# A vision tower, a two-way state-space layer and a mixture of experts in one kernel: three image pairs in flight per loop pass, both images of a pair in one instruction, and B and C rows spread by DMA

## The reference, cut to what matters

```python
x = patch_embed(images)                     # 16x16 patches: 196 tokens and a class token, 128 channels
for l in range(2):                          # two transformer layers, 8 heads of 16
    h = rmsnorm(x, ln1)
    attn = softmax((q @ k.T) / 4)           # 197 x 197 per head
    x = x + (attn @ v) @ wo.T
    h2 = rmsnorm(x, ln2)
    x = x + (silu(h2 @ wg.T) * (h2 @ wu.T)) @ wd.T   # 344 wide
h = rmsnorm(x, ln_f)
# state-space layer, forward and backward in time, 16 states per channel
dA  = exp(dt[..., None] * A)
dBx = dt[..., None] * Bm[:, :, None, :] * xs[..., None]
hst = scan(dA, dBx)                         # h[t] = dA[t] * h[t-1] + dBx[t]
y   = (einsum('blds,bls->bld', hst, Cm) + D * xs) * silu(z)
h = layernorm(h + out_f + out_b)
# 64 experts, 8 per token, at most 256 tokens per expert over the whole batch
h = layernorm(h + moe(h))
```

## Time and profile before

| what | value |
|---|---|
| median of 3 runs | 12895.33 us (12876.94 to 12912.05) |
| profiled execution, span from first to last instruction | 13032.3 us |
| median over span | 0.9895 |
| DVE busy over the span | 8016.1 us, 62% |
| PE busy over the span | 8924.6 us, 68% |
| ACT busy over the span | 5903.0 us, 45% |
| POOL busy over the span | 2489.9 us, 19% |
| mean granted PE clock, share of full speed | 0.779 |

### The profile page before, as it was taken

One profiled execution on the slowest core, in us unless ns is written; L12 is line 12 of the kernel. 1 busy time (PEld: TensorE's weight loads), 2 busy tenths in 40 slices (PEclk: granted clock), 3 DMA queues, 4 the chain that ended last, 5 costly groups with the idle time before them and its releaser, 6 DMA issues. The chain is left out here.

```text
span 13032.3 us, 153093 instructions
## 1 busy us (share of the span) xinstructions
PE 8924.6 (68%) x48772; PEld 5897.0 (45%) x48772; DVE 8016.1 (62%) x13143; ACT 5903.0 (45%) x13164; POOL 2489.9 (19%) x1809
## 2 busy tenths in 40 slices
PE   5656566577777777777777777777777777777642
PEld 3434344344444444444444444444444444444421
DVE  3556566566666666666666666666666666666724
ACT  4334343444544454445444544445444544454411
POOL 0222222211111111111111111111111111111164
PEclk8777777787878888878878887878787878888755
DMA  2000000000000000000000000000000000000034
GB/s 88 7 11 6 12 6 8 10 10 5 10 10 10 5 10 10 10 6 9 10 10 10 5 10 10 10 5 10 10 10 5 10 10 10 6 9 10 2 53 111
DMA packets 130841, 183.68 MB, mean 14 GB/s; under 512 B 27033, under 2 KB 112893, under 8 KB 121469
## 3 DMA queue, kind: packets, MB, share of 16 engines
q1 hardware_dynamic: 95068, 150.00, 3.6%
q0 software_dynamic: 34816, 21.19, 1.2%
HBM read 113.96 MB, written 57.12 MB: 13 GB/s over the span
## 5 line engine op out<-in xcount | busy, mean ns | idle before, releaser
L478 POOL TENSOR_TENSOR hs<-hs 128x788 f32<-128x788 f32 x512 | 949.7, 1855 | 7866.3 <-DVE hs L904 7866.3
L608 ACT ACTIVATE P<-psS,least_s 99x197 f32<-99x197 f32 x4096 | 1394.7, 428 | 1437.9 <-DVE least_s L791 1437.0
L1109 PE MATMUL psS<-KM,Q 128*99 128x394 f32 x4096 | 1757.9, 549 | 162.0 <-issue 61.9
L897 DVE TENSOR_TENSOR_SCAN hs<-dA,hs 128x1576 f32<-128x1576 f32 x512 | 1763.9, 3445 | 27.5
L1123 PE MATMUL psS<-cst,P 99*99 99x99 f32 x8192 | 1108.5, 288 | 818.9 <-ACT P L608 762.8
L692 ACT ACTIVATE dA<-dt_,aneg 128x394 f32<-128x394 f32 x2048 | 1179.4, 617 | 682.5 <-DVE hs L897 682.5
L1123 PEld LDWEIGHTS psS<-cst,P 99*99 99x99 f32 x8192 | 963.7, 194 | 1133.1 <-ACT P L608 1047.3
L1219 PE MATMUL psA<-bc,bcsel_h 96*128 96x394 bf16 x2048 | 786.1, 384 | 800.4 <-DVE hs L904 624.0
L791 DVE TENSOR_REDUCE least_s<-psS 99x4 f32<-99x788 f32 x1024 | 991.2, 973 | 278.6 <-PE psS L1109 265.7
L1109 PEld LDWEIGHTS psS<-KM,Q 128*99 128x99 f32 x4096 | 729.7, 187 | 703.9 <-issue 536.0
L575 ACT ACTIVATE sq<-X 128x197 f32<-128x197 f32 x640 | 228.5, 366 | 1780.3 <-DVE X L824 1140.3
(11 more groups left out here) (203 smaller groups left out, 15631.5 us busy)
## 6 DMA issues: line engine op xcount, KB each, us to landing
pat<-patches SPq DMA_DIRECT2D x64, 1176.0 KB
rows_scratch<-zeros SPq DMA_DIRECT2D x1, 19104.0 KB, 61.9
hs<-sum_scratch SPq DMA_DIRECT2D x24, 512.0 KB, 3.5
out<-hs SPq DMA_DIRECT2D x24, 512.0 KB, 2.6
sum_scratch<-HW SPq DMA_DIRECT2D x64, 148.5 KB
slot_scratch<-toki,sloti POOLq DMA_INDIRECT x320
dA<-w SPq DMA_DIRECT2D x32, 128.0 KB
sum_scratch<-HW SPq DMA_DIRECT2D x64, 48.5 KB
```

Source lines behind the costliest of these rows:

```text
L478: nc.gpsimd.tensor_tensor(hs[:, g % HBUF, 0:2, :], hs[:, g % HBUF, 0:2, :], hs[:, g % HBUF, 2:4, :], ALU.add).then_inc(half_summed, 1)
L608: last = nc.scalar.activation(P[:, b, m, 0:T], psS[0:CT, 2 * b + m // 2, m % 2 * T:(m % 2 + 1) * T], ACT.Exp, bias=least_s[:, b, m:m + 1], ...
L897: nc.vector.tensor_tensor_scan(h, dA[:, g % 2, :, :].rearrange("p n t -> p (n t)"), h, 0.0, ALU.mult, ALU.add).then_inc(scan_ready, 1)
L1109: last = mm(psS[0:CT, 2 * b + j, 0:2 * T].rearrange("p (e t) -> p e t", e=2), Q[:, b, q * CT:(q + 1) * CT], KM[:, b, m:m + 2, 0:T], start= ...
```

## The change

The diff rewrites the main loop; the experts and the closing norm keep their work and their order.

1. **Three pairs per pass.** The front half is cut into two roles. Role 0 does patch embedding and layer 0 of one pair, role 1 does layer 1 and the last norm of the pair before it, and the units do the state-space layer of the pair before that. `role_stages` lists a role's stages; the 101 stages of both are merged by position, role 1 with a lag of 2.5 stages. X has three buffers, and the other tensors of the front half are indexed by role instead of by image.
2. **Merged images.** Stages outside the attention rounds handle both images in one instruction (394 columns for 197). A role has eight rounds of two heads and a half of the queries, still one image at a time, so that each instruction of a round is half as wide: one score matmul of 394, a minimum over 2x197, two exponentials, four transposes, a copy of 396. The count of score matmuls, exponentials and transposes over a pass stays.
3. **B and C by DMA.** `xproj` is one matmul with 64 output rows (32 for dt, 32 for B and C). Its B and C rows are written to DRAM (`share`, SP queue), and each group's four B rows and four C rows are read back to all 128 partitions by one DMA each (`load`). The selector matmuls and `split` are gone. Inputs and outputs are one DVE instruction of 4x394 per group.
4. **Sums.** The first addition of a group moves from POOL to DVE (`half`); the second is now a second identity matmul on PE.
5. **Masked keys** are made on ACT as 16 copies of 396 with a per-partition scale (`keys`), not on DVE and POOL.
6. **Tables.** New `WEIGHT` and `COST`, the same for all engines. By `shares()` the first input unit stands behind stage 43 of 101 (counted from 0); everything up to the eighth decay of a pass stands before it, the eight scans, outputs and halves and seven of the eight inputs after it.

```diff
+UNITS = [("patch",), ("project", 0, 0), ("-sum", QUARTERS - 1), ("project", 0, 1), ("project", 1, 0), ("conv", 0), ("-ys", 1),
+         ("project", 1, 1), ("-merge",), ("keep",), ("conv", 1), ("sigmoid", 0), ("leave",), ("-route",), ("-store",),
+         ("sigmoid", 1), ("gate", 0), ("gate", 1), ("xproj", 0), ("share", 0), ("load", 0), ("load", 1), ("xproj", 1),
+         ("share", 1), ("load", 2), ("dtproj", 0), ("dt", 0), ("dtproj", 1), ("dt", 1)]
+UNITS += [("decay", g, k) for g in range(2) for k in range(QN)] + [("input", 0)]
 for _g in range(QUARTERS):
-    for _k in range(QN):
-        UNITS += [("decay", 1, _k)] if _g == 0 else []
-        UNITS += [("input", _g, _k)]
-    UNITS += [("scan", _g)] + ([("sum", _g - 1)] if _g else [])
-    for _k in range(QN):
-        UNITS += [("decay", _g + 2, _k)] if _g + 2 < QUARTERS else []
-        UNITS += [("output", _g, _k)]
...
-COST = {"project": 2, "conv": 2, "sigmoid": 2, "gate": 3, "xproj": 2.55, "split": 2.88, "dtproj": 0.65, "dt": 4,
-        "decay": 0.3, "input": 0.5, "scan": 2, "output": 0.5, "sum": 0.61, "merge": 4, "keep": 0.3, "leave": 0,
...
+def role_stages(r):
+    out = [("conv", 0)] if r == 0 else []
+    out += [("square", r, 0), ("norm", r, 0), ("qkv", r), ("keys", r, 0)]
+    for n in range(ROUNDS):
+        out += [("score", r, n, b) for b in range(G)]
+        out += [("keys", r, n + 1)] if n + 1 < HP else []
+        out += [("value", r, 0)] if n == HP else []
+        out += [("turn", r, n, b) for b in range(G)]
+    out += [("value", r, 1), ("den", r), ("wo", r), ("square", r, 1), ("norm", r, 1), ("gate", r), ("sig", r), ("up", r), ("down", r)]
+    out += [("square", r, 2), ("norm", r, 2)] if r else []
+    return out
...
+LAG = 2.5
...
+        "input": 1.7, "scan": 3.4, "half": 0.9, "output": 1.7, "sum": 0.6, "ys": 1, "merge": 4, "keep": 0.3, "leave": 0,
...
+                for k, (name, r, *args) in enumerate(STAGES):
+                    i = (ahead, front)[r]
+                    if i is not None and name in stages:
+                        stages[name](i, r, *args)
+                    if back is not None:
+                        until(SHARE[k])
+            run(0, None, None)
+            run(1, 0, None)
+            run(2, 1, 0)
+            with eng.Fori(0, STEPS - 3 - peel) as i:
+                run(i + 3, i + 2, i + 1)
+            for i in range(STEPS - 2 - peel, STEPS - 2):
+                run(i + 2, i + 1, i)
+            run(None, STEPS - 1, STEPS - 2)
...
+            def share(i, d):
+                if d == 0 and not is_first(i):
+                    q.wait_ge(mul_done, i * MULS)
+                    q.sem_inc(q_waited, 1)
+                if d == 0:
+                    q.wait_ge(xs_ready, i * 2 + 2)
+                    q.sem_inc(q_waited, 1)
+                q.wait_ge(dtbc_ready, i * 2 + d + 1)
+                q.dma_start(bc_d[d], dtbc[DTR:DTR + 2 * NS, d, :]).then_inc(bc_stored, 16)
...
+            def load(i, g):
+                d, n = divmod(g, QUARTERS // 2)
+                if n == 0:
+                    q.wait_ge(bc_stored, i * 32 + d * 16 + 16)
+                    q.sem_inc(q_waited, 1)
+                if g >= HBUF or not is_first(i):
+                    q.wait_ge(acc_done, i * QUARTERS + g - HBUF + 1 if g >= HBUF else i * QUARTERS)
+                q.dma_start(hs[:, g % HBUF, :, :], bc_d[d:d + 1, n * QN:(n + 1) * QN, :].to_broadcast([128, QN, N])).then_inc(b_loaded[g % HBUF], 16)
+                if g >= CBUF or not is_first(i):
+                    q.wait_ge(mul_done, i * MULS + MUL_OUT[g - CBUF] if g >= CBUF else i * MULS)
+                q.dma_start(cr[:, g % CBUF, :, :], bc_d[d:d + 1, NS + n * QN:NS + (n + 1) * QN, :].to_broadcast([128, QN, N])).then_inc(c_loaded[g % CBUF], 16)
             q.sem_inc(hw_free, 1)
...
-            def sum_(i, g):
-                pool.wait_ge(mul_done, i * MULS + (g + 1) * 2 * QN)
-                nc.gpsimd.tensor_tensor(hs[:, g % HBUF, 0:2, :], hs[:, g % HBUF, 0:2, :], hs[:, g % HBUF, 2:4, :], ALU.add).then_inc(half_summed, 1)
-                pool.wait_ge(half_summed, i * QUARTERS + g + 1)
-                nc.gpsimd.tensor_tensor(hs[:, g % HBUF, 0, :], hs[:, g % HBUF, 0, :], hs[:, g % HBUF, 1, :], ALU.add).then_inc(summed, 1)
...
+            def keys(i, r, h):
+                act.wait_ge(kq_done[r], i * 2 + 1)
+                for k in (2 * h, 2 * h + 1):
+                    last = nc.scalar.activation(KM[:, r, k, :, :].rearrange("p g t -> p (g t)"), psG[:, r, 0:2 * TP], ACT.Copy, scale=c("heads", k, k + 1))
+                last.then_inc(km_ready[r], 1)
...
+            def turn(i, r, n, b):
+                h = n % HP
+                act.wait_ge(round_done[r], i * ROUNDS * 4 + n * 4 + 2 + b + 1)
+                nc.scalar.activation(PT[:, r, b, 2 * h:2 * h + 2, :, :].rearrange("p h c t -> p (h c t)"), psS[0:CT, 2 * r + b, 0:2 * TP], ACT.Copy).then_inc(p_ready[r], 1)
...
-            def input_(i, g, k):
-                m = 2 * QN * g + k
-                if k == 0 and g >= HBUF:
-                    dve.wait_ge(acc_done, i * QUARTERS + g - HBUF + 1)
-                dve.wait_ge(bb_done, i * MULS + m + 1)
-                nc.vector.tensor_tensor(hs[:, g % HBUF, k, :], u[:, g // (QUARTERS // 2), :], AB[m % 2][:, 0:N], ALU.mult).then_inc(mul_done, 1)
+                nc.vector.tensor_tensor(u[:, d, :], dt_[:, d, :], XZ[:, d, 0, :], ALU.mult).then_inc(u_ready, 1)
+            def input_(i, g):
+                d = g // (QUARTERS // 2)
+                dve.wait_ge(b_loaded[g % HBUF], ring(i, g, HBUF))
+                dve.wait_ge(u_ready, i * 2 + d + 1)
+                nc.vector.tensor_tensor(hs[:, g % HBUF, :, :], hs[:, g % HBUF, :, :], u[:, d, :].unsqueeze(1).to_broadcast([128, QN, N]), ALU.mult).then_inc(mul_done, 1)
...
-            def output(i, g, k):
-                m = 2 * QN * g + QN + k
-                if k == 0:
-                    dve.wait_ge(scan_ready, i * QUARTERS + g + 1)
-                dve.wait_ge(bb_done, i * MULS + m + 1)
-                nc.vector.tensor_tensor(hs[:, g % HBUF, k, :], hs[:, g % HBUF, k, :], AB[m % 2][:, 0:N], ALU.mult).then_inc(mul_done, 1)
...
+            def output(i, g):
+                dve.wait_ge(scan_ready, i * QUARTERS + g + 1)
+                dve.wait_ge(c_loaded[g % CBUF], ring(i, g, CBUF))
+                nc.vector.tensor_tensor(hs[:, g % HBUF, :, :], hs[:, g % HBUF, :, :], cr[:, g % CBUF, :, :], ALU.mult).then_inc(mul_done, 1)
+            def half(i, g):
+                dve.wait_ge(mul_done, i * MULS + MUL_OUT[g])
+                nc.vector.tensor_tensor(hs[:, g % HBUF, 0:2, :], hs[:, g % HBUF, 0:2, :], hs[:, g % HBUF, 2:4, :], ALU.add).then_inc(half_summed, 1)
...
+            def score(i, r, n, b):
+                q, h = divmod(n, HP)
+                if n == 0:
+                    (pe.wait_ge(q_ready[r], i + 1), pe.wait_ge(v_ready[r], i + 1))[b]
+                else:
+                    pe.wait_ge(p_ready[r], i * ROUNDS * 4 + (n - 1) * 4 + 2 + b + 1)
+                if q == 0 and b == 0:
+                    pe.wait_ge(km_ready[r], i * HP + h + 1)
+                mm(psS[0:CT, 2 * r + b, 0:2 * T].rearrange("p (e t) -> p e t", e=2), Q[:, r, b, q * CT:(q + 1) * CT], KM[:, r, 2 * h:2 * h + 2, b, 0:T], start=True, stop=True).then_inc(round_done[r], 1)
...
-            def broadcast(i, g, m, row):
-                d = g // (QUARTERS // 2)
-                if m == 0:
-                    pe.wait_ge(bcs_ready, i * 2 + 2)
-                if m >= 2:
-                    pe.wait_ge(mul_done, i * MULS + m - 1)
-                mm(AB[m % 2][:, 0:N], bcsel[:, row, :], bc[:, d, :], start=True, stop=True).then_inc(bb_done, 1)
...
             def sum_(i, g):
                 d, q = divmod(g, QUARTERS // 2)
                 if q == 0:
                     pe.wait_ge(dt_ready, i * 2 + 2) if d == 0 else pe.wait_ge(ys_ready, i * 2 + 1)
-                pe.wait_ge(summed, i * QUARTERS + g + 1)
-                mm(psY[:, 0:N], c("ident"), hs[:, g % HBUF, 0, :], start=q == 0, stop=False).then_inc(acc_done, 1)
+                pe.wait_ge(half_summed, i * QUARTERS + g + 1)
+                for k in range(2):
+                    last = mm(psY[:, 0:N], c("ident"), hs[:, g % HBUF, k, :], start=q == 0 and k == 0, stop=False)
+                last.then_inc(acc_done, 1)
                 if q == QUARTERS // 2 - 1:
```

804 lines of the change are left out of this document (330 added, 474 removed), and 3 rows, old and new, of the table WEIGHT.

## The result

| | before | changed |
|---|---|---|
| median | 12898.8 us (12876.94 to 12912.05) | 12477.15 us (12476.19 to 12479.61) |
| ratio | | 0.9673, 95% interval 0.9659 to 0.9687 |
| span of the profiled execution | 13032.3 us | 12477.3 us |
| steady pass | 184.32 us | 180.91 us |
| mean granted PE clock | 0.779 | 0.778 |

The kernel is 3.3% faster. The direction was predicted, the size was not: 12477 us lies above the range that ended at 12200.

A forecast was written before the change was run, and what follows sets the result against it. Waits between engines, none of them full, were taken as the bound. Sections of 55 and 95 us gave passes of 150; 211 + 63 x 150 + 486 + 724 - 15 = 10856, at 0.9895 10742 us, range 9800 to 12200.

The forecast's parts named there:

- landing within 5 us: Sign that the forecast is right: each B or C load by DMA lands within 5 us of issue.
- three (loads): Rival: the 16 loads per pass on one queue become the bound; at 15 us each, 16.35 ms, chance 0.06.
- four (clock): Rival: PE at half clock throughout, pass of 194 us, 13.48 ms, chance 0.04.
- +7: Stages 0 to 42: 7 us for ACT partly idle in the chain ahead of the rounds, on 48 us of work.
- I add 7: Stages 43 to 100: 7 us for waits from softmax sums to layer end, on 88 us of DVE work.
- so rounds are well covered: Attention rounds: DVE waited only 16.8 us for scores over five passes; the stages around them were not covered.
- DVE's work: Count of DVE's work per pass: 118.6 becomes 118 us, with 7.8 us for the additions taken from POOL.
- PE's work: Count of PE's work per pass: 91 us at full clock, about 110 at 0.80; eight new identity matmuls 5.3 us.
- Second rival: Waits between engines only move: 66 us idle stays, pass of 184 us, 12.9 ms, chance 0.05.
- two chains of half the length are now filled by each other: Argument against waits merely moving: the two roles' half-length chains fill each other's gaps; no size given.
- First rival: DVE's work alone bounds the pass: 126 us per pass, 9245 us in all, chance 0.07.
- The factor 0.9895: Whole kernel: ratio of run median to profiled span (12895.33 over 13032.3), turning a span of 10856 into 10742 us.

The follow-up runs named there:

- half_first: Changed kernel with DVE's addition put ahead of the scan instead of behind it; 11977.84 us, 0.9098 of the kernel before.
- lag4_5: `sum_late` with LAG 4.5 in place of 2.5; 11386.56 us, 0.8643 of the kernel before.
- thin: `sum_late` with DVE's inputs, scans, outputs and halves done for one state in four, output wrong; 10714.75 us.
- split_prep: `lag5_5` with DVE's part of each sigmoid, gate and step size made its own unit behind ACT's part; 11464.82 us, ratio 0.8695.
- one_sum: Changed kernel with one of the two identity matmuls of each group left out, output incomplete; 12354.65 us, ratio 0.9389.
- filled: `lag5_5` with one more matmul of 198 columns on PE ahead of each group of transposes; 11899.89 us.
- both: Changed kernel with the edits of `half_first` and `sum_late` together; 11669.69 us, 0.9062 of the kernel before.
- lag5_5: `sum_late` with LAG 5.5 in place of 2.5; 11377.37 us, 0.8841 of the kernel before.
- lag_only: Changed kernel with only LAG 5.5 in place of 2.5; 12107.86 us, 0.9431 of the kernel before.
- sum_late: Changed kernel with PE's identity matmuls put behind the next input; 11898.02 us, 0.9037 of the kernel before.
- pool_sums: Changed kernel with both additions on POOL and one identity matmul per group; 12413.98 us, 0.9432 of the kernel before.
- thin_lag: `thin` with LAG 5.5 in place of 2.5; 10521.76 us.
- thin_more: `thin_lag` with 24 of the 32 decays on ACT left out too; 10095.98 us.

## Why the prediction was wrong

- **The work of DVE**, 118 us per pass forecast, 114.0 measured; inputs and outputs 1.80 forecast, 1.79 measured. Right within the 5 us named. **ACT**: 97 forecast, 91.5 measured. **The clock**: 0.80 kept, 0.79 measured. **The loads**: forecast at nothing and 4.5 us each; they landed in 7.1 (B) and 4.1 us (C), and DVE waited 0.0 us for them, so the sign "landing within 5 us" failed for B without a cost. **PE**: the 91 us at full clock come to 114 at 0.80, not to "about 110"; recorded are 625.0 / 5 = 125.0, with overlaps. Rivals three (loads) and four (clock) did not happen.
- **The step that failed** is the pair of terms for waits, "+7" in stages 0 to 42 and "I add 7" in stages 43 to 100. By the sections as measured they are 64.3 - 37.6 = 27 us beside ACT, and 116.6 - 83.8 = 33 us beside DVE: 60 where 14 stood. The work in them was 10 us and 4 us below the forecast: 150 + 46 - 14 = 182, measured 180.9.
- They rested on "so rounds are well covered", read from 16.8 us of idle time ahead of L791. That was a row of the old order. The change halved each round's work per meeting, so the meetings doubled, and it moved the addition from POOL, on which no minimum waits, into DVE's line behind the scan, with PE's `sum` right behind it. Under "DVE's work" and "PE's work" I priced this move as 7.8 us on DVE and 5.3 us on PE and never asked what is queued behind the waiting instruction: 17.8 us of PE idle, paid for with 10 us per pass by `half_first`. Another 7 us per pass are the order of the two roles (LAG). Of the 31 us by which the pass missed 150, the best steady pass measured with the same work on every engine (160.4, `lag4_5`) takes back 20; the remaining 10 have no run of their own.
- **Second rival**, "the waits only move", had it: 66.9 us idle against 66. It named a pass of 184, measured were 180.9, which is 184 less the 3 to 4 us that DVE's work fell. The sign I had named for it, some 60 us of idle time spread over the rounds, is what the groups show. That waits in turns and not an engine's work set the pass, and that a wait taken away turns up elsewhere, is what `thin` and `split_prep` show. Its mechanism, twice as many meetings, fits them, but no run changed the number of meetings. I gave it 0.05 because of the argument that "two chains of half the length are now filled by each other"; the runs with LAG show that how well they fill each other depends on the exact order and had to be looked at.
- **First rival**, DVE alone as the bound, is excluded by `thin`, where 41 us less of its work gave 15. PE's work as the bound (theory 2) is spoken against by `half_first`, `one_sum` and `filled` together.
- **The passes with the expert choice**: I left their 486 us as they were. They fell to 162, counted with the last pass, and so did more for the result than the steady pass did. Over a steady pass an expert pass took 17 us more in `both` and `thin`, 19 in the changed kernel, 22 in `lag5_5` and `lag_only`, but 34 in `half_first`, `sum_late` and `pool_sums` and about 40 in `filled`, `split_prep` and `thin_lag`; what sets it was not tried alone and stays open.
- **The rest of the sum.** Start and tail held (207 for 211, 711 for 724). The factor 0.9895 did not: the kernel before had been profiled in an execution 1% slower than its runs, and in the changed kernel the median is 12477.15 for a span of 12477.3. With the measured pass and all else as forecast the sum is 211 + 63 x 180.91 + 486 + 724 - 15 = 12803, times 0.9895 = 12669 us. So the pass was short by 1947 us in all, and the expert passes took back a part of that.

What stays open in the steady pass: the 140 us of `thin_more` were not split further, and why certain orders fit better than others is seen only as a result. The best version measured, later identity matmuls and LAG 5.5, takes 11377 us: 8.8% less than the changed kernel (11377 / 12480 = 0.912), 0.8841 of the kernel before; LAG 4.5 is as good (11387 us).

## What to carry to other kernels

When engines run fixed lists in order, price a moved instruction by what stands ahead of it and who waits behind it, not by its length: a 0.96 us addition behind a 3.44 us scan cost 10 us per pass, and one line moved it away. Idle time in rows of the old order did not tell of the meetings in the new one; list, for the longest instruction of each engine, which other engine needs the instruction behind it. Before working on a wait that the profile names, take away work beside it: if the pass moves by much less than the work (15 us for 41 here), waits in turns set the pace, and the order of the chain is the next thing to try. And where a loop has passes of two kinds, read both: several totals here moved by what happened in some ten of 64 passes.

## What the runs showed of the hardware

- GpSimd and DVE, each with two operands in SBUF, slowed each other as if they took turns for whole instructions: an addition of 394 elements took 3.89 us beside a scan (0.88 us in the kernel before, in a place beside other work), and the scan 4.13 instead of 3.44 us.
- Steady passes of the changed kernel repeat to 0.02 us (180.91), those of the kernel before are 184.32 us with some of 185.6 and 186.4 between; in `lag5_5` they go between 160.8, 163.4 and 164.0 us. A pass of one length is not a given even where the program is the same.
- B and C loads are of one size (788 KB) and from one place. In the changed kernel B loads took 7.1 us from issue to landing and C loads 4.1, as shown here; in `lag5_5` they took 4.1 and 4.3, in `both` 4.0 and 4.1:

```profile
hs<-bc_scratch SPq DMA_DIRECT2D x512, 788.0 KB, 7.1
cr<-bc_scratch SPq DMA_DIRECT2D x512, 788.0 KB, 4.1
```

So the time of the same load differs between orders of the same work; what shared the queues then was not tried.
